# From block 3 on q is made of seven quarter products in the outputs' banks, and a block opens in another order

## What is computed

```python
xn = layernorm(x)                                  # x: 4 x 1024 x 1024, f32
h = rmsnorm(xn) * qkv_norm_w
q, k, v = split(h @ ternary(qkv_w).T)              # 16 heads of 64
# in chunks of T = 128 tokens, S is a head's 64 x 64 state
scores = (q @ k.T) * mask                          # mask[t, s] = exp(-s_h (t - s)), t >= s
o = scale * (scores @ v + (q * lam_t) @ S)
S = lam_T * S + (k * lam_rev).T @ v
s = rmsnorm(rmsnorm(o) * norm_w) * proj_norm_w @ ternary(proj_w).T
g = silu(xn @ ternary(ffn_w).T + ffn_b)
out = x + s * g
```

## Time and profile before

| | before |
|---|---|
| median of 3 runs | 1304.9 us (1303.99 to 1307.63) |
| profiled execution, its time | 1304.94 us |
| its span | 1303.7 us |
| PE busy | 1271.8 us, 98% |
| DVE busy | 998.4 us, 77% |
| ACT busy | 741.1 us, 57% |
| POOL busy | 518.2 us, 40% |
| project_qk's matmuls (L866) | 2432 in the whole kernel, 1664 of them in blocks 3 to 15 |
| granted TensorE clock | 0.997 over the span |

### The profile page before, as it was taken

The page is one execution under the profiler, slowest core; times in us unless marked ns, Lnnn a source line. Parts: engine busy times, 40 slices in busy tenths (PEclk is TensorE's granted clock), DMA queues, the critical chain, the costliest instruction groups (busy, mean ns, idle before and its releaser), DMA issues.

```text
span 1303.7 us, 26389 instructions
## 1 busy us (share of the span) xinstructions
PE 1271.8 (98%) x10263; PEld 806.5 (62%) x10263; DVE 998.4 (77%) x1552; ACT 741.1 (57%) x1792; POOL 518.2 (40%) x435
## 2 busy tenths in 40 slices
PE   4999999999999999999999999999999999999998
PEld 2576867666665746657565665757566574656655
DVE  7888368677777878789777787878878787878745
ACT  5886256273554646566464566657456464646732
POOL 1430793835434334253432235242243324325161
PEclk9999999999999999999999999999999999999999
DMA  9622211303113031130402103040120404112020
GB/s 360 254 98 74 58 50 34 114 10 106 49 34 113 18 106 34 39 116 18 138 18 89 42 22 133 17 136 20 73 66 17 130 17 127 29 48 75 2 81 33
DMA packets 35677, 97.69 MB, mean 75 GB/s; under 512 B 10977, under 2 KB 11233, under 8 KB 35554
## 3 DMA queue, kind: packets, MB, share of 16 engines
q1 hardware_dynamic: 33024, 88.65, 19.8%
q10 hardware_dynamic: 2530, 7.37, 2.7%
HBM read 71.85 MB, written 16.81 MB: 68 GB/s over the span
## 4 chain that ended last, share of the span: by engine, by line
PE 85%; POOL 4%; DVE 4%; issue 3%; ACT 2%; DMA 1%; SPq 0%; DVEq 0%; POOLq 0%; ACTq 0%
PE ring L866 18%; PE ring L825 13%; PE ring L799 13%; PE ring L851 12%; PE ring L1030 10%; PE att_ps L904 4%; PE ring L1006 3%; PE att_ps L959 3%; PE ring L916 2%; PE att_ps L932 2%; PE att_ps L962 1%; DVE b_lo L1438 1%; PE ring L769 1%; DMA raw<-in_ffn_w 1%; POOL ffn_sum L2452 1%
## 5 line engine op out<-in xcount | busy, mean ns | idle before, releaser
L866 PE MATMUL ring<-b_hi,qkv_q 128*128 128x256 f16 x1216 | 268.2, 272 | 0.8 <-DVE b_lo L1438 0.8
L866 PE MATMUL ring<-b_lo,qkv_q 128*128 128x256 f16 x1216 | 268.2, 273 | 0.0
L2557 POOL TENSOR_TENSOR xt<-xt,gate_even 128x512 f32<-128x512 f32 x58 | 90.1, 1557 | 205.8 <-DVE gate_even L1626 158.0
L2535 POOL TENSOR_TENSOR sq<-sq 128x512 f32<-128x512 f32 (+1 forms) x58 | 58.0, 1000 | 239.8 <-DVE b_lo L1438 143.7
L866 PEld LDWEIGHTS ring<-b_hi,qkv_q 128*128 128x128 fp8e4 x1216 | 120.2, 99 | 17.9 <-DVE b_lo L1438 1.7
L866 PEld LDWEIGHTS ring<-b_lo,qkv_q 128*128 128x128 fp8e4 x1216 | 118.9, 98 | 14.9
L2161 ACT ACTIVATE sq<-att_ps,sq_scale 128x128 f32<-128x128 f32 x256 | 69.9, 381 | 54.3 <-DVE ow L1581 29.7
L2056 ACT ACTIVATE arena<-arena,lam_T 64x64 f32<-64x64 f32 x384 | 93.0, 329 | 4.3 <-issue 3.7
L2546 POOL TENSOR_TENSOR small<-small 128x1 f32<-128x1 f32 x32 | 19.6, 614 | 162.2 <-DVE small L1633 162.2
L2523 POOL TENSOR_TENSOR stack_odd<-arena,lam_q 64x1024 f32<-64x1024 f32 x32 | 82.6, 2581 | 2.9 <-POOL xt L2557 0.3
L2077 ACT ACTIVATE gate_odd<-ring,wscale 128x512 f32<-128x512 f32 x26 | 17.9, 687 | 112.0 <-PE ring L851 112.0
(11 more groups left out here) (305 smaller groups left out, 3561.8 us busy)
## 6 DMA issues: line engine op xcount, KB each, us to landing
xt<-in_x SPq DMA_DIRECT2D x60, 512.0 KB, 4.0
out<-xt SPq DMA_DIRECT2D x31, 512.0 KB, 2.6
raw<-in_qkv_w SPq DMA_DIRECT2D x24, 512.0 KB, 15.8
arena<-arena ACTq DMA_DIRECT2D x28, 256.0 KB, 2.9
y<-in_x_turned SPq DMA_DIRECT2D x14, 512.0 KB, 5.8
y_odd<-in_x_turned SPq DMA_DIRECT2D x14, 512.0 KB, 6.7
raw<-in_ffn_w SPq DMA_DIRECT2D x8, 512.0 KB, 10.0
norm_rows<-norm_out SPq DMA_DIRECT2D x14, 256.0 KB, 5.9
```

What stands on the lines that cost most here:

```text
L866: ins = pe.matmul(ring[:, b, e * BT:(e + 1) * BT], qkv_q[:, cb, o:o + P], part[:, cb, :], start=(cb == 0 and part is b_hi and (e == 0 or i ...
L2535: pool.tensor_tensor(sq[:, 0, 0:m, :], sq[:, 0, 0:m, :], sq[:, 0, m:2 * m, :], ALU.add).then_inc(s_sqw, 1)
L2557: pool.tensor_tensor(o, o, gate_of(i)[:, c, cs], ALU.add).then_inc(s_add, 1)
```

## The change

q is made by seven products too, from block 3 on. A product q_product(i, name) holds a 128 x 128 piece of the (summed) weights and moves 128 tokens' part of b, high and then low: 4 pieces of outputs x 4 of channels x 2 halves = 32 matmuls of 128 columns. It writes to the banks of the attention's outputs: p1, p2 in att_bank(0), p5, p3 in att_bank(1), and p6, p7, p4 in a bank of the ring. v's p1 and o's p5 move to the outputs' banks as well. ACT and DVE get for q what they have for k: begin_q_bank, begin_q, take_q, add_q. POOL makes T1 to T4 for q in blocks 0 to 2. S3 of b is kept in the place of a quarter (1, 0) that is no longer split (one high_b and one split_b of four pieces fewer a block). weigh_b is cut in halves, and the orders of PE, DVE and ACT at the opening of a block are new. sq_sum is one tile instead of two.

```diff
             ring_uses += [...]   # behind a block with o products
-                ring_uses += [("qk", i, 0), ("qk", i, 1), ("qk", i, 2), ("held", i - 1, 0), ("qk", i, 3)]
-                ring_uses += [("k product", i, "p1"), ("k product", i, "p5"), ("held", i - 1, 1)]
-                ring_uses += [("k product", i, "p6"), ("o product", i - 1, "p5")]
+                ring_uses += [("k product", i, "p1"), ("k product", i, "p6"), ("q product", i, "p6"), ("held", i - 1, 0)]
+                ring_uses += [("k product", i, "p5"), ("k held", i), ("q held", i), ("held", i - 1, 1)]
...
+            def q_product(i, name):
...
+                if name == "p1":
+                    pe.wait_ge(s_blo, of_b_half(i, 1, 1))
+                    pe.wait_ge(s_sq, HALF * chunk(i, 0))
+                elif name in ("p2", "p6"):
+                    pe.wait_ge(s_qseed, i - BY_TOKENS + 1)
+                elif name == "p3":
+                    pe.wait_ge(s_qbase, 2 * (i - BY_TOKENS) + 1)
+                elif name == "p7":
+                    pe.wait_ge(s_qbase, 2 * (i - BY_TOKENS) + 2)
+                elif name == "p4":
+                    pe.wait_ge(s_qsum, of_q_pair(i, 1))
+                of, w = b_pair_of(part), q_weights_of(weights)
+                to = q_bank(i, name).rearrange("p (m t) -> p m t", m=CPH)
+                for m in range(CPH):
+                    for j in range(CPH):
+                        for k in range(2):
+                            ins = pe.matmul(to[:, m, :], w[:, j, m * P:(m + 1) * P], of[:, k, j, :],
...
 # PE, opening of blocks 3 to 15
-                project_qk(i, 0)
-                project_qk(i, 1)
+                q_product(i, "p1")
+                k_product(i, "p1")
                 output_scale(i - 1, 1)
-                project_qk(i, 2)
+                q_product(i, "p2")
+                k_product(i, "p2")
                 spread_gamma(i - 1, 1)
-                project_qk(i, 3)
-                k_product(i, "p1")
+                q_product(i, "p5")
+                k_product(i, "p5")
+                q_product(i, "p6")
+                k_product(i, "p6")
                 if by_products(i - 1):
-                    k_product(i, "p5")
                     o_product(i - 1, "p6")
-                    k_product(i, "p2")
-                    k_product(i, "p6")
+                    q_product(i, "p3")
+                    k_product(i, "p3")
                     o_product(i - 1, "p7")
-                    k_product(i, "p3")
+                    q_product(i, "p7")
                     k_product(i, "p7")
                     o_product(i - 1, "p5")
+                    q_product(i, "p4")
+                    k_product(i, "p4")
+                    o_product(i - 1, "p4")
                     v_product(i, "p1")
+                    o_product(i - 1, "p3")
...
 # DVE, end of a block, and opening of the next
                     split_b(i + 1, 0, 1)
-                    split_b(i + 1, 1, 0)
                     split_b(i + 1, 1, 1)
                     take_z21(i)
                     if not last:
                         add_state(i, 1)
-                    gate_out(i, 0, 0)
...
-                for name in Y_SUMS:
-                    sum_b(i, name)
+                sum_b(i, "S1")
+                sum_b(i, "S3")
+                if by_products(i - 1):
+                    gate_out(i - 1, 0, 0)
+                sum_b(i, "S2")
                 output_scale(i - 1, 1)
-                for name in Y_SUMS:
-                    low_b_sum(i, name)
+                sum_b(i, "S4")
+                low_b_sum(i, "S1")
+                low_b_sum(i, "S2")
                 scale_o(i - 1, 1)
+                low_b_sum(i, "S4")
+                low_b_sum(i, "S3")
                 if by_products(i - 1):
                     for name in O_ROWS:
                         sum_o(i - 1, name)
-                    low_o_part(i - 1, "a22")
-                    low_o_part(i - 1, "S2")
+                    for name in O_PARTS:
+                        low_o_part(i - 1, name)
+                    add_q(i, 0)
                     if more:
                         norm_stats(i + 1, 1)
-                    for name in ("S3", "S1", "S4"):
-                        low_o_part(i - 1, name)
+                    add_k(i, 0)
...
 # ACT, opening
+                weigh_b(i, 1, 0)
+                weigh_b(i, 1, 1)
+                weigh_b(i, 0, 0)
+                begin_q_bank(i)
+                weigh_b(i, 0, 1)
+                high_b_sum(i, "S1")
+                begin_k_bank(i)
                 if by_products(i - 1):
+                    silu(i - 1, 1, 0)
+                take_q(i, 0)
+                high_b_sum(i, "S2")
+                take_k(i, 0)
+                high_b_sum(i, "S4")
+                high_b_sum(i, "S3")
+                if by_products(i - 1):
+                    begin_q(i, 1)
+                    begin_k(i, 1)
+                    high_o_part(i - 1, "S2")
+                    begin_q(i, 0)
                     high_o_part(i - 1, "a22")
+                    begin_k(i, 0)
                     high_o_part(i - 1, "S3")
+                    begin_out(i - 1, 0)
                     high_o_part(i - 1, "S1")
                     high_o_part(i - 1, "S4")
+                    high_part(i, "a22")
+                    high_part(i, "a11")
+                    begin_out(i - 1, 1)
+                    high_part(i, "a12")
                     high_part(i, "S1")
                     high_part(i, "S3")
                     high_part(i, "S2")
+                    take_q(i, 1)
                     high_part(i, "S4")
```

More of the change, by code:

```diff
@@ L298, in of_projected, with o_bank @@
             return of_half(i, c, h) if i < BY_PRODUCTS else of_half(BY_PRODUCTS, c, h)
+        def o_bank(i, name):
+            if SHARED[name] == "p5":
+                return att_bank(1)
+            return ring[:, bank_of("o product", i, SHARED[name]), :]
         def o_row_of(name):
@@ L824, in v_product @@
                     for k, of in enumerate(b_part_of(part)):
-                        ins = pe.matmul(ring[:, b, :], of[:, j, :], v_weights_of(weights)[:, j, :],
+                        ins = pe.matmul(to, of[:, j, :], v_weights_of(weights)[:, j, :],
                                         start=(name in ("p1", "p5") and j == 0 and k == 0),
@@ L866, in project_qk @@
                             ins = pe.matmul(ring[:, b, e * BT:(e + 1) * BT], qkv_q[:, cb, o:o + P], part[:, cb, :],
-                                            start=(cb == 0 and part is b_hi and (e == 0 or i < BY_TOKENS)),
-                                        stop=(cb == NCB - 1 and part is b_lo), skip_group_check=True)
+                                            start=(cb == 0 and part is b_hi), stop=(cb == NCB - 1 and part is b_lo))
                 ins.then_inc(s_qk, 1)
@@ L1915, in vector_program @@
                         norm_stats(i + 1, 1)
+                    low_part(i, "a22")
+                    sum_y(i, "S1")
+                    gate_out(i - 1, 1, 0)
+                    add_q(i, 0)
                     sum_y(i, "S3")
+                    add_k(i, 0)
                     low_part(i, "a11")
+                    add_q(i, 1)
                     sum_y(i, "S2")
-                    gate_out(i - 1, 1, 0)
+                    add_k(i, 1)
                     low_part(i, "a12")
+                    gate_out(i - 1, 1, 1)
                     sum_y(i, "S4")
@@ L2329, in scalar_program @@
                     high_part(i, "a12")
-                    weigh_b(i, 0)
-                    weigh_b(i, 1)
+                    for c in (1, 0):
+                        weigh_b(i, c, 0)
+                        weigh_b(i, c, 1)
                 if i > 0:
@@ L2335, in scalar_program @@
                         if i > 1 and j == 4:
-                            for name in Y_SUMS:
+                            for name in B_PARTS[:3]:
                                 high_b_sum(i, name)
+                        if i > 1 and j == PR - 1:
+                            high_b_sum(i, B_PARTS[3])
                         if i > 1 and j in (1, 2):
```

315 lines of the change are left out of this document (195 added, 120 removed).

## The result

| | before | changed |
|---|---|---|
| median | 1306.27 us (4 runs, 1303.99 to 1309.15) | 1338.79 us (4 runs, 1337.60 to 1339.12) |
| ratio | 1 | 1.0231 (95% interval 1.0204 to 1.0258) |
| span of the profiled execution | 1303.7 us | 1337.4 us |
| PE busy, share of the span | 98% | 94% |
| mean granted clock | 0.997 | 0.987 |

The change makes the kernel slower: by 2.3% as a ratio, by 32.5 us from median to median. Forecast were 1314 us and a range up to 1333: the sign is right, the size is far too small, and the time lies outside the range.

A forecast was written before the change was run, and what follows sets the result against it. The prediction took the kernel as bound by the columns PE streams, any PE wait costing its full length. 1304.9 - 19.2 (columns) + 13.3 (openings) + 13 (middle) + 2.6 (blocks 3, 4) - 0.4 (one wait gone) = 1314 us, range 1293 to 1333.

The forecast's parts named there:

- The columns: q products on PE in blocks 3 to 15: fewer streamed columns, 1.78 us a product, -19.2 us in all.
- rival (c): q products on PE: weight loads don't hide under 128 columns, 77 ns a matmul, 1348 us; chance 0.10.
- The openings: Start of blocks 5 to 15: q p2 and k p2 wait for bank copies behind gate_out, +13.3 us.
- The middle: Middle of blocks 5 to 14: norm_stats 4.5 us later delays centring; PE waits 1.3 us a block, +13 us.
- Blocks 3 and 4: Turned loads come later because high_part S4 stands behind take_q(1): about as much as in later blocks, +2.6 us.
- POOL's sums: Four q weight sums of 3.83 us in blocks 0 to 2 lie in POOL's idle stretches: 0, at worst +2 us.
- The ends: Whole kernel: the range from 1293 to 1333 us, leaving out about 0.17 of the chances.

The follow-up runs named there:

- e4: The changed kernel with norm_stats(i+1, 1) put back ahead of the third low part of o in blocks 5 to 14: 1329.1 us, ratio 1.0147.
- e7: The changed kernel with one edit: in blocks 2, 3 and 4 POOL holds its decays and sums until the second centring is made: 1328.7 us, ratio 1.0136.
- b1: The kernel before with two more POOL sums in block 0, where the changed kernel has T1 and T2: 1316.8 us, ratio 1.0049.
- e2: The changed kernel; in blocks 3 and 4 high part S4 precedes take_q(1), sum S4 and low parts precede gate_out(i-1, 1, 1): 1330.5 us, ratio 1.0162.
- e6: all5 with one more wait: in blocks 2, 3 and 4 POOL holds its decays and sums until the second centring is made: 1287.7 us, ratio 0.9836.
- all5: The changed kernel with the five edits of e1, e2, e3, e4 and e5 together: 1298.8 us, ratio 0.9914.
- e5: The changed kernel with DVE's gate_out(i-1, 0, 0) ahead of norm_stats(i+1, 0) and sums S1 and S3 of b in blocks 5 to 15: 1332.2 us, ratio 1.0173.
- e1: The changed kernel with POOL's q sums T1, T2 and T4 placed later in its order: 1336.0 us, ratio 1.0209.
- e3: The changed kernel with centre(3, 0) ahead of the low part S3 of b on DVE in block 2: 1341.8 us, ratio 1.0248.

## Why the prediction was wrong

- **The columns (-19.2 us): right.** 1.79 us a product, and 14.0 us in ten blocks once nothing waits. The weight loads hide under 128 columns: rival (c) is out. The Trainium skill (TensorE: Matmul & The Clock Gate, "Back-to-back issue gap") has about 81 ns a matmul at 128 columns; the trace has 56.
- **The openings (+13.3): right, in size too.** The waits list 8.1 + 2.4 = 10.5 us; by starts it is more. In block 10 the first matmul of o p6 starts at +15.8, as forecast, where the products ahead of it end at +14.4 if nothing waits, and over blocks 5 to 15 this distance sums to 13.9 us. gate_out comes within 0.03 us of its walk. Blocks 8 and 12 are 1.6 us shorter where 0.6 longer was forecast: their q p2 is late by 0.1 (0.8 was booked for the opening), k p2 by 0.4, a wait of 0.4 that before had at its spread of gamma is gone, and the middle, booked with 1.3 in each of ten blocks, has no wait there.
- **The middle (+13): right in mechanism, two thirds in size.** The waits are L1015 3.2, L1003 2.1 (the other 0.4 is in block 0) and 1.3 of L890's: 6.6 us listed in eight of the ten blocks. By starts it is 9.0, which is also what e4 gives back by moving the statistics alone. It grows with the store's landing, to which e7 owes 7 us more. Together blocks 5 to 15 came to +5.4 where the terms give -16.3 + 13.3 + 13 = +10; most of the distance is this term.
- **Blocks 3 and 4 (+2.6): the step that failed worst.** They came to +17.3 although the columns give back 3.0: a cost of 20.3 us. The step saw that high_part S4 stands behind take_q(1) and the turned load behind the low part S4, and then put "about as much" as in the steady blocks, without walking it through. In block 3 the load came at +41.35, 14.7 later than before, not 4.5. e7 parts it: without POOL's share, and with the new order, the load is issued at +33.4, 6.7 later, and the centring takes 4.9 us; then no wait for add_v is left.
- **POOL's sums ("0, at worst +2"): failed, +7.5 in block 0.** The step took POOL's idle time as proof of a free place and asked only whether POOL itself had time, not who else is slow while POOL works. b1 gives the price: +7.1 in block 0.
- **Block 2 (+3.1): not costed at all.** S3 of b moved into a quarter that block 2's project_qk still reads; its low part, and the centring behind it in DVE's queue, wait for the last of these. It stands in the change and in no term. This delay alone costs nothing: in e7, where S3 stands as in the changed kernel and only POOL waits, block 2 has no wait for add_v and lasts 80.9 us.
- **The ends.** The range had no term for blocks 0 to 4 but +2 and +2.6, so that its upper end, 1333, couldn't hold what these blocks did.

What the three misses have in common can be read in the trace of before. Centring is 2.26 and 2.19 us in the earlier trace rows where "short" ones take 1.2, and the prediction took that for a thing that may go either way. It has a cause: POOL's adds to the residual ran there (1.26 us from 863.08, 2.13 from 868.22). The rounding, the low parts and the centring on DVE read only SBUF and take 0.68 to 1.23 us by themselves; beside POOL one goes for each of POOL's operations. The shorter ones end 0.55 us behind the POOL operation that they met (4.31 beside 4.16 and 2.84 beside 2.69 in block 0), the centring 1.1 behind (338.2 for POOL's 337.1 in e2). The Trainium skill (SBUF — State Buffer, "SBUF: two separate sides") says that DVE and GpSimd share one pair of ports under an exclusive lock: it concerns a DVE operation in a 2-port perf mode or with two SBUF inputs, whichever starts first holds the pair for its whole length, and the other blocks fully. The trace agrees in the lengths, also for operations that this condition leaves out: the four mask operations read a bank of PSUM, and in block 2 of the changed kernel they keep their 2.46 us together although POOL decays until 267.64. DVE, then POOL:

```profile
266.01 2.46 DVE L1633 TENSOR_TENSOR arena<-att_ps,mask 64x512 f32<-64x512 f32 x4
```

```profile
261.15 6.49 POOL L2684 TENSOR_TENSOR stack_odd<-arena,lam_q 64x1024 f32<-64x1024 f32 x2
```

That the slow operations come from POOL is shown by b1 and e6; that a port lock is the reason is the skill's account, which no run here tests by itself.

What stays open is the 13 us by which all5 exceeds its parts. In that sum the changed kernel's ratio counts four times, each with an interval of 0.0027 either way, so that the 0.0101 is not clear of noise. The profiled executions give 17.4 us: 6.5 of it is the opening's gain that e5 lost again in blocks 5 to 14, 8.6 is that these blocks happened to be 2.8 to 2.9 us longer in e1, e2 and e3, and the rest, mostly in blocks 1 to 4, wasn't taken apart.

## What to carry to other kernels

An idle stretch of POOL is a place for its work only if DVE has no operation on the critical path there that reads only SBUF: each such operation that met POOL here cost the length of POOL's. Look for groups on DVE whose longest is several times the shortest, and ask what POOL did then; here one POOL wait was worth 0.8% on all5, and 0.4% on the kernel before. And where a change gives a new order to a queue, walk the special blocks at the start through as carefully as the steady ones: 28 of 34 us were lost there, while the change itself, with five orders put right and POOL held back, is worth 1.6%, or 1.3% against the kernel before with the same POOL wait (0.9836 by 0.9962).

## What the runs showed of the hardware that was not expected

- DVE rounding operations of 0.74 us take 4.31 us beside POOL sums of 4.16 (b1: 4314 ns at most) and 2.84 beside a decay of 2.69, and an f16 low part of 0.68 takes 2.83 beside a decay of 3.12 (e3); four centring operations 13.1 us with POOL and 4.9 without (e2, e6).
- A straight line from 256 and 512 columns holds down to 128: 56 ns, with a weight load for each matmul.
- After a hole of 10.3 us PE's first matmuls of 512 columns were 0.43 us apart instead of 0.216: half the clock, and the granted clock of that block is 0.94. The same hole of 3.7 us in block 2 left the clock of the block at 1.00 in the changed kernel's profile and at 0.98 in those of e2 and e3, which made it 1.7 us longer.
- Two executions of one kernel can differ by 6.5 us (1304.94 and 1311.44) with nearly the same mean clock (0.997 and 0.996): two waits of 1.6 and 3.0 us that one has and the other hasn't, and the lower clock behind the second.
